# A DLRM tower on one core: pair banks spread between other matmuls, and the low halves of the tables made in two pieces with waits

## Chip, core and metric

The kernel runs on one core of a Trainium2 chip. The metric is the device time of one execution in microseconds (us). Five engines work side by side, each through its own list of instructions: TensorE (PE), VectorE (DVE), ScalarE (ACT), GpSimd (POOL) and SyncE (SP). They wait for one another through semaphores.

## What is computed

For 2048 samples, 27 embedding rows of 128 floats are looked up, the 351 dot products of each sample's rows are taken, 16 dense features are put behind them, and a small network of three layers follows.

```python
e = jnp.stack([tbl_0[ids[:, 0]], ..., tbl_26[ids[:, 26]]], axis=1)   # 2048 x 27 x 128
xactions = jnp.einsum('bfd,bgd->bfg', e, e)
z = xactions[:, _TRIL_I, _TRIL_J].reshape(2048, -1)                   # 351 pairs
h = jnp.concatenate([z, dense_ctx], axis=1)                           # 367
h = jnp.maximum(h @ W_top1 + b_top1, 0.0)                             # 512
h = jnp.maximum(h @ W_top2 + b_top2, 0.0)                             # 256
y = h @ W_top3
```

The tables have 1000, 1250, 12500 or 125000 rows.

## The kernel before

The 2048 samples are 16 tiles of 128, in 8 groups of 2 tiles (256 samples). A group passes through these steps; the list `STEPS`, written out by `order()` (L66), sets their order on every engine.

- **hot**: the 10 or 11 smallest tables are looked up by matmuls. Each such table lies in SBUF in chunks of 128 rows (8 chunks for the first five, 10 for the others). VectorE makes a one-hot matrix of 128 x 256 for each chunk (`make_one_hots`, L763) and TensorE multiplies it with the chunk (`look_up`, L510 and L511). For full precision a table is held as a high part and a low part, and each chunk takes two matmuls. ScalarE makes the high part (`make_high`, L632) and VectorE the low part, as table minus high part (`make_low`, L738). Both are made once, during group 0: for each table VectorE makes the low part and then the one-hots of group 0, in two halves, the second of which waits for the first (`hot_made`). The one-hots go into a ring of 20.
- **cold**: the other tables' rows are fetched from HBM by GpSimd, one indirect DMA for a tile and a table (L471, 260 in all), transposed by TensorE four at a time (L493), and copied by ScalarE (L639) into `et`, where the hot results go too (L651).
- **pairs**: the dot products of 64 samples are one "pair bank" of 64 matmuls of 26 columns (`row_pairs`, L526). A group has 4 pair banks, which use two PSUM banks in turn: a bank may start when the bank before the last has been moved out. Each bank has 4 strips, which ScalarE and VectorE copy out in shares set by `strips_of` (L410), 4 copies to a strip. The banks 0 and 1 need tile 0 of the group, 2 and 3 need tile 1.
- **layer1, layer2, layer3** of the group before: 12 (L540), 8 (L559) and 4 (L576) matmuls, with ScalarE's relus between (L657, L666). Before layer1 some of the pair results are moved to their places by DMAs that SyncE issues (`complete_zt`, L369), 14 and one for the dense features. For the last group they are split by tile between SyncE and GpSimd (8 and 7 or 7 and 8 for a tile), and layer1 runs tile by tile (L550).

An fp32 matmul of the program is two records in the trace, each with a weight load, so a pair bank is 128 matmul records and 128 loads. In group 0 there is no earlier group, and tile 1's cold steps and the pair banks 1 to 3 come among the first hot steps of group 1. In the last group the layer1 of the group before stands among the pair banks.

## Time and profile before

| | us |
|---|---|
| median of 3 executions | 388.83 |
| lowest, highest | 386.91, 1133.02 |
| the profiled execution | 386.78 |
| its span, first to last instruction | 385.0 |
| PE, DVE, ACT, POOL busy | 351.8, 272.6, 231.8, 274.3 |

The profiled execution lies 2 us under the median of the three and 0.1 under the lowest. The span misses 1.8 us of its time, which lie ahead of the first and behind the last instruction. Times in the rows below count from the start of the span. An idle time stands in brackets behind a row, with what ended it; "issue" says that the profile shows nothing that the engine waited for.

### The profile page before, as it was taken

What the parts mean: (1) busy time and instruction counts of PE and PEld (TensorE: products, weight loads), DVE (VectorE), ACT (ScalarE), POOL (GpSimd) and SP (SyncE); (2) the same over time, 40 slices, a digit from 0 to 9 for tenths busy, and PEclk for the clock granted to TensorE, in tenths of its full rate; (3) what the DMA queues carried; (4) which work ended last, traced back from release to release, by engine and by line L of the source; (5) the groups of instructions that cost most, each with busy time, mean ns of one, the idle gap of its engine ahead of it and who ended that gap; (6) DMA issues with size and microseconds to landing.
All of it is one profiled execution on the core that took longest, in us unless ns stands there. A gap on an engine that the chain in (4) does not pass through costs nothing.

```text
span 385.0 us, 15124 instructions
## 1 busy us (share of the span) xinstructions
PE 351.8 (91%) x6340; PEld 327.9 (85%) x6340; DVE 272.6 (71%) x1052; ACT 231.8 (60%) x504; POOL 274.3 (71%) x283
## 2 busy tenths in 40 slices
PE   0857796999999999999999999999999999998798
PEld 0856685998899989998999989998889989997687
DVE  2999997794679827894779737894679938894421
ACT  3468255944658465754768465753848555777543
POOL 4878877777777777777777777777777777783340
PEclk9999999999999999999999999999999999999899
DMA  7977243253132533225232533234222512221000
GB/s 267 382 226 232 72 135 112 82 173 93 50 85 56 165 85 78 59 63 152 51 84 53 155 83 81 55 76 161 55 82 54 159 52 58 52 60 32 8 10 2
DMA packets 20675, 38.39 MB, mean 100 GB/s; under 512 B 7040, under 2 KB 9536, under 8 KB 20608
## 3 DMA queue, kind: packets, MB, share of 16 engines
q0 software_dynamic: 8800, 17.12, 16.8%
q1 hardware_dynamic: 9824, 17.42, 13.9%
q10 hardware_dynamic: 1984, 2.89, 2.3%
q8 instruction: 50, 0.82, 0.9%
q14 instruction: 17, 0.14, 0.1%
HBM read 36.53 MB, written 0.01 MB: 95 GB/s over the span
## 4 chain that ended last, share of the span: by engine, by line
PE 66%; POOL 13%; issue 8%; DVE 6%; DMA 3%; SPq 3%; ACT 1%; DVEq 0%
PE fill_ps L510 15%; PE fill_ps L511 15%; POOL rows L471 13%; PE pair_ps L526 11%; PE mlp_ps L540 9%; PE fill_ps L493 5%; PE mlp_ps L559 5%; DVE one_hot L763 4%; SPq L369 3%; DVE table_lo L738 2%; DMA work<-tbl_d 2%; PE fill_ps L550 1%; DMA rows<-tbl_d,ids_sb 1%; PE mlp_ps L510 1%; PE mlp_ps L511 1%
## 5 line engine op out<-in xcount | busy, mean ns | idle before, releaser
L471 POOL DMA_INDIRECT rows<-tbl_d,ids_sb x260 | 265.9, 1023 | 82.8 <-issue 75.9
L763 DVE TENSOR_SCALAR one_hot<-hot_ids 128x256 fp32r<-128x256 f32 x780 | 187.1, 304 | 25.1 <-PE fill_ps L511 13.4
L510 PE MATMUL fill_ps<-one_hot,table_hi 128*128 128x256 f32 x748 | 187.2, 290 | 16.3 <-DVE one_hot L763 16.0
L511 PE MATMUL fill_ps<-one_hot,table_lo 128*128 128x256 f32 x748 | 182.8, 285 | 0.0
L510 PEld LDWEIGHTS fill_ps<-one_hot,table_hi 128*128 128x128 f32 x748 | 144.6, 193 | 18.1 <-issue 15.5
L511 PEld LDWEIGHTS fill_ps<-one_hot,table_lo 128*128 128x128 f32 x748 | 144.8, 194 | 0.2
L410 ACT COPY work<-pair_ps 26x112 f32<-26x112 f32 (+1 forms) x280 | 66.7, 238 | 51.7 <-PE pair_ps L526 48.6
L410 DVE COPY work<-pair_ps 26x112 f32<-26x112 f32 (+1 forms) x168 | 43.3, 258 | 52.2 <-PE pair_ps L526 50.2
L639 ACT COPY et<-fill_ps 128x512 f32<-128x512 f32 (+1 forms) x68 | 75.2, 1241 | 4.2 <-PE fill_ps L493 3.9
L651 ACT COPY et<-fill_ps 128x512 f32<-128x512 f32 (+1 forms) x44 | 49.6, 1161 | 43.1 <-PE fill_ps L511 39.3
L526 PEld LDWEIGHTS pair_ps<-et 128*26 128x26 f32 x4096 | 45.6, 103 | 23.5 <-issue 15.0
L526 PE MATMUL pair_ps<-et 128*26 128x26 f32 x4096 | 54.2, 192 | 12.1 <-issue 6.3
L540 PE MATMUL mlp_ps<-work,w_sb 128*128 128x256 f32 x168 | 39.2, 390 | 0.2 <-DMA work<-dense_d 0.2
L493 PE MATMUL fill_ps<-ident,rows 128*128 128x128 f32 x260 | 35.4, 276 | 2.8 <-ACT et L651 1.3
L540 PEld LDWEIGHTS mlp_ps<-work,w_sb 128*128 128x128 f32 x168 | 32.3, 196 | 4.8 <-DMA work<-dense_d 0.4
L493 PEld LDWEIGHTS fill_ps<-ident,rows 128*128 128x128 f32 x260 | 28.7, 141 | 4.3 <-DMA rows<-tbl_d,ids_sb 3.6
L748 DVE TENSOR_SCALAR hot_ids<-hot_ids,first_row 128x512 f32<-128x512 int32 (+1 forms) x54 | 23.8, 452 | 3.9 <-DMA hot_ids<-ids_hot_d 3.9
L559 PE MATMUL mlp_ps<-work,w_sb 128*128 128x256 f32 x112 | 26.3, 379 | 0.0
L657 ACT ACTIVATE work<-mlp_ps,vectors 128x256 f32<-128x256 f32 x28 | 11.8, 471 | 23.5 <-PE mlp_ps L540 23.5
L559 PEld LDWEIGHTS mlp_ps<-work,w_sb 128*128 128x128 f32 x112 | 20.3, 190 | 2.3
L369 POOL DMA_DIRECT2D hot_ids<-hot_ids x14 | 7.1, 514 | 15.1 <-ACT hot_ids L410 10.9
L410 DVE COPY hot_ids<-pair_ps 26x112 f32<-26x112 f32 (+1 forms) x32 | 8.3, 258 | 11.9 <-PE pair_ps L526 11.5
(41 smaller groups left out, 112.4 us busy)
## 6 DMA issues: line engine op xcount, KB each, us to landing
hot_ids<-ids_hot_d SPq DMA_DIRECT2D x34, 256.0 KB, 4.1
rows<-tbl_d,ids_sb POOLq DMA_INDIRECT x260, 4.1
work<-tbl_d SPq DMA_DIRECT2D x5, 640.0 KB, 4.1
work<-tbl_d SPq DMA_DIRECT2D x4, 512.0 KB, 7.2
hot_ids<-ids_hot_d ACTq DMA_DIRECT2D x6, 256.0 KB, 7.2
w_sb<-w_d ACTq DMA_DIRECT2D x5, 256.0 KB
hot_ids<-ids_hot_d SPq DMA_DIRECT2D x6, 128.0 KB, 3.9
w_sb<-tbl_d SPq DMA_DIRECT2D x1, 640.0 KB, 4.0
```

The costliest lines, as they stand in the source:

```text
L410: last = copy(homes_of_pairs[g][STRIP * q:STRIP * q + PAIR_COLS, place(q + 1)[1]:, at:at + BANK_ROWS], frm[:, q::STRIPS, :])
L471: nc.gpsimd.indirect_dma_start(out=rows[:, t, c, :], out_offset=None, in_=tables[f], in_offset=bass.IndirectOffsetOnAxis(ap=ids_sb[:, tile ...
L493: last = nc.tensor.transpose(bank[:, c * P:(c + 1) * P], rows[:, t, c0 + c, :], ident[:, :])
L510: nc.tensor.matmul(to, table_hi[:, CHUNK_AT[k] + c, :], hot, start=(c == 0), stop=False)
L511: last = nc.tensor.matmul(to, table_lo[:, CHUNK_AT[k] + c, :], hot, start=False, stop=(c == CHUNKS_OF[k] - 1))
L526: last = nc.tensor.matmul(pair_ps[bank % 2][32 * s:32 * s + PAIR_COLS, r * PAIR_COLS:(r + 1) * PAIR_COLS], et[:, row, 0:FEATURES - 1], et[ ...
L540: last = nc.tensor.matmul(mlp_psum(m), w1_sb[:, c, m * P:(m + 1) * P], zt[g][:, c, :], start=(c == 0), stop=(c == CHUNKS - 1))
L559: last = nc.tensor.matmul(mlp_ps[m][:, 0:COLS], w2_sb[:, c, m * P:(m + 1) * P], h1[:, c, :], start=(c == 0), stop=(c == K2 - 1))
L639: nc.scalar.copy(et[:, t * P:(t + 1) * P, c0:c0 + n].rearrange("p r f -> p f r"), fill_psum(step)[:, 0:n * P].rearrange("p (f r) -> p f r" ...
L651: nc.scalar.copy(et[:, :, slot:slot + n].rearrange("p r f -> p f r"), fill_psum(step)[:, 0:n * COLS].rearrange("p (f r) -> p f r", f=n)).t ...
L748: nc.vector.tensor_scalar(ids.bitcast(F32), ids, first_row[:, n:n + 1], None, ALU.subtract).then_inc(hot_ids_local, 1)
L763: last = nc.vector.tensor_scalar(one_hot[:, (first + c - c0) % ONE_HOT_RING, :], ids, float(c), None, ALU.is_equal)
```

## The change

It has three parts.

1. `order()`: the steps are written so that no two pair banks follow one another. In group 0, hot step 1 of group 1 moves from between the cold steps to between pair banks 2 and 3. In the last group, the layer1 of the group before is cut into four steps of 3 matmuls, one behind each pair bank; before, it was two steps of 6, behind banks 1 and 3. Layer1 is called by quarters in the other groups too, where the order stays as it was; it signals `h1_full` four times rather than twice, and ScalarE's relus wait for the same matmuls as before.
2. `strips_of`: in the last group bank 1 is shared 2 and 2 strips, where VectorE had 1 and ScalarE 3.
3. `make_low`: each table's low part is made in two halves. VectorE waits ahead of the first until its one-hots so far are finished, between the halves until the first is finished, and behind them until the second is finished. The count of `lo_made` doubles for all who wait on it.

```diff
         if b == 0:
-            steps += [hot[0]] + first_cold[:2] + [("pairs", b, 1), first_cold[2], hot[1]] + first_cold[3:]
-            steps += [("pairs", b, 2), ("pairs", b, 3)]
+            steps += [hot[0]] + first_cold[:2] + [("pairs", b, 1)] + first_cold[2:]
+            steps += [("pairs", b, 2), hot[1], ("pairs", b, 3)]
...
         else:
-            steps += cold[1] + [("pairs", g, 0), ("pairs", g, 1), ("layer1", b, 0), ("pairs", g, 2), ("pairs", g, 3)]
-            steps += [("layer1", b, 1), ("layer2", b, 0), ("layer2", b, 1)]
+            steps += cold[1]
+            for bank in range(PAIR_BANKS):
+                steps += [("pairs", g, bank), layer1[bank]]
+            steps += [("layer2", b, 0), ("layer2", b, 1)]
...
-        shares = {"dve": (3, 1, 2, 2), "act": (1, 3, 2, 2)}
+        shares = {"dve": (3, 2, 2, 2), "act": (1, 2, 2, 2)}
...
-                nc.vector.tensor_tensor(table_lo[:, c0:c1, :], raw_table(k), table_hi[:, c0:c1, :].bitcast(F32),
-                                        ALU.subtract).then_inc(lo_made, 1)
+                for half, (c0, c1) in enumerate(halves(k)):
+                    at = slice(CHUNK_AT[k] + c0, CHUNK_AT[k] + c1)
+
+                    wait_count(dve, hot_made, 2 * min(k, N_HOT[0]))
+                    wait_count(dve, lo_made, 2 * k + half)
+                    nc.vector.tensor_tensor(table_lo[:, at, :], raw_table(k)[:, c0:c1, :],
+                                            table_hi[:, at, :].bitcast(F32), ALU.subtract).then_inc(lo_made, 1)
+                wait_count(dve, lo_made, 2 * k + 2)
```

On TensorE, in the last group, these rows stood between the last transposes and the tile-by-tile layer1 (`pair_ps` are the two banks of the pairs, `mlp_ps` those of the layers):

```order
L526 MATMUL pair_ps0<-et 26x26 x64
L526 MATMUL pair_ps1<-et 26x26 x64
L540 MATMUL mlp_ps0<-work,w1_sb 128x256 x6
L526 MATMUL pair_ps0<-et 26x26 x64
L526 MATMUL pair_ps1<-et 26x26 x64
L540 MATMUL mlp_ps1<-work,w1_sb 128x256 x6
L559 MATMUL mlp_ps0<-work,w2_sb 128x256 x4
L559 MATMUL mlp_ps1<-work,w2_sb 128x256 x4
```

and these stand there now:

```order
L529 MATMUL pair_ps0<-et 26x26 x64
L542 MATMUL mlp_ps0<-work,w1_sb 128x256 x3
L529 MATMUL pair_ps1<-et 26x26 x64
L542 MATMUL mlp_ps0<-work,w1_sb 128x256 x3
L529 MATMUL pair_ps0<-et 26x26 x64
L542 MATMUL mlp_ps1<-work,w1_sb 128x256 x3
L529 MATMUL pair_ps1<-et 26x26 x64
L542 MATMUL mlp_ps1<-work,w1_sb 128x256 x3
L560 MATMUL mlp_ps0<-work,w2_sb 128x256 x4
L560 MATMUL mlp_ps1<-work,w2_sb 128x256 x4
```

The matmuls are the same; every bank has 3 of layer1 behind it.

On TensorE, in group 0, these rows stood between pair bank 1 and hot step 2 of group 1 (hot step 1, which writes `mlp_ps1`, is 16 chunks of two rows each, of which the first is shown):

```order
L526 MATMUL pair_ps1<-et 26x26 x64
L493 MATMUL fill_ps0<-ident,rows 128x128 x4
L510 MATMUL mlp_ps1<-one_hot,table_hi 128x256
...
L493 MATMUL fill_ps1<-ident,rows 128x128 x4
L493 MATMUL fill_ps2<-ident,rows 128x128
L526 MATMUL pair_ps0<-et 26x26 x64
L526 MATMUL pair_ps1<-et 26x26 x64
```

and now:

```order
L529 MATMUL pair_ps1<-et 26x26 x64
L496 MATMUL fill_ps0<-ident,rows 128x128 x4
L496 MATMUL fill_ps1<-ident,rows 128x128 x4
L496 MATMUL fill_ps2<-ident,rows 128x128
L529 MATMUL pair_ps0<-et 26x26 x64
L513 MATMUL mlp_ps1<-one_hot,table_hi 128x256
...
L529 MATMUL pair_ps1<-et 26x26 x64
```

The 9 transposes of tile 1 stand together, and the hot step has moved behind pair bank 2.

On VectorE, in the start, one table of 10 chunks was (`hot_ids` are the ids that a one-hot is made from; each instruction's waits stand behind it):

```order
L738 TENSOR_TENSOR table_lo<-work,table_hi 128x1280 [waits hi_made,raw_in2]
L763 TENSOR_SCALAR one_hot<-hot_ids 128x256 [waits hot_made,hot_used,hot_ids_local]
L763 TENSOR_SCALAR one_hot<-hot_ids 128x256 x4
L763 TENSOR_SCALAR one_hot<-hot_ids 128x256 [waits hot_made,hot_used]
L763 TENSOR_SCALAR one_hot<-hot_ids 128x256 x4
```

and are now:

```order
L744 TENSOR_TENSOR table_lo<-work,table_hi 128x640 [waits hot_made,lo_made,hi_made,raw_in2]
L744 TENSOR_TENSOR table_lo<-work,table_hi 128x640 [waits lo_made,hot_made]
L770 TENSOR_SCALAR one_hot<-hot_ids 128x256 [waits hot_used,hot_made,hot_ids_local,lo_made]
L770 TENSOR_SCALAR one_hot<-hot_ids 128x256 x4
L770 TENSOR_SCALAR one_hot<-hot_ids 128x256 [waits hot_made,hot_used]
L770 TENSOR_SCALAR one_hot<-hot_ids 128x256 x4
```

One subtraction has become two of half its width, and the first one-hot now waits for `lo_made` as well.

## Rows read from the trace of the kernel before

**Rows 1.** The page: busy time and instructions, and the queue that loads instructions.

```profile
PE 351.8 (91%) x6340; PEld 327.9 (85%) x6340; DVE 272.6 (71%) x1052; ACT 231.8 (60%) x504; POOL 274.3 (71%) x283
...
q8 instruction: 50, 0.82, 0.9%
```

**Rows 2.** Busy time by stretch: length, then us and count for PE, PEld, DVE, ACT, POOL.

```profile
271.00:314.00 43.00, 42.48 (x788) 39.78 (x787) 31.54 (x127) 26.30 (x59) 32.94 (x34) 1.00 0.30 83
```

**Rows 3.** Waits: who for whom, us in total, times, longest.

```profile
PE fill_ps L510 <- DVE one_hot L763: 16.0, 5, 10.5
```

**Rows 4.** Timeline of VectorE in the start: start, us, engine, line, operation.

```profile
24.80 1.48 DVE L738 TENSOR_TENSOR table_lo<-work,table_hi 128x1280 fp32r<-128x1280 f32 x1
26.20 2.46 DVE L763 TENSOR_SCALAR one_hot<-hot_ids 128x256 fp32r<-128x256 f32 x10
28.58 1.48 DVE L738 TENSOR_TENSOR table_lo<-work,table_hi 128x1280 fp32r<-128x1280 f32 x1
...
46.30 0.70 DVE L786 MEMSET work<- 128x768 f32 x1 [0.23 <-PE fill_ps L511]
```

**Rows 5.** Groups of instructions by form: busy us, mean ns, idle before.

```profile
L738 DVE TENSOR_TENSOR table_lo<-work,table_hi 128x1024 fp32r<-128x1024 f32 x4 | 4.9, 1237 | 2.6 <-ACT table_hi L632 2.6
```

**Rows 6.** Timeline of GpSimd in the start.

```profile
28.65 2.22 POOL L471 DMA_INDIRECT rows<-tbl_d,ids_sb  x1 [0.30 <-issue]
31.18 0.94 POOL L471 DMA_INDIRECT rows<-tbl_d,ids_sb  x1 [0.30 <-issue]
```

**Rows 7.** Timeline of TensorE: the two waits for a gather after the start.

```profile
99.11 0.66 PE L493 MATMUL fill_ps<-ident,rows 128*128 128x128 f32 x4 [0.24 <-DMA rows<-tbl_d,ids_sb]
...
351.88 0.66 PE L493 MATMUL fill_ps<-ident,rows 128*128 128x128 f32 x4 [0.29 <-DMA rows<-tbl_d,ids_sb]
```

**Rows 8.** Timeline of TensorE: pair banks 2 and 3 of group 0.

```profile
62.81 2.64 PE L526 MATMUL pair_ps<-et 128*26 128x26 f32 x189 [1.41 <-ACT et L639]
67.55 0.92 PE L526 MATMUL pair_ps<-et 128*26 128x26 f32 x67 [2.10 <-issue]
68.40 0.38 PE L510 MATMUL fill_ps<-one_hot,table_hi 128*128 128x256 f32 x1
```

**Rows 9.** Timeline of ScalarE ahead of them: the cold copies of tile 1.

```profile
53.83 1.22 ACT L639 COPY et<-fill_ps 128x512 f32<-128x512 f32 x1 [2.39 <-PE fill_ps L493]
54.80 1.27 ACT L639 COPY et<-fill_ps 128x512 f32<-128x512 f32 x1
58.61 1.22 ACT L639 COPY et<-fill_ps 128x512 f32<-128x512 f32 x1
61.34 1.43 ACT L639 COPY et<-fill_ps 128x512 f32<-128x512 f32 x2 [1.51 <-PE fill_ps L493]
```

**Rows 10.** Timeline of TensorE: the pair banks of the last group.

```profile
352.46 2.04 PE L526 MATMUL pair_ps<-et 128*26 128x26 f32 x214
356.89 0.71 PE L526 MATMUL pair_ps<-et 128*26 128x26 f32 x42 [2.40 <-issue]
357.53 4.22 PE L540 MATMUL mlp_ps<-work,w_sb 128*128 128x256 f32 x12
361.69 2.72 PE L526 MATMUL pair_ps<-et 128*26 128x26 f32 x201
365.60 0.65 PE L526 MATMUL pair_ps<-et 128*26 128x26 f32 x55 [1.19 <-issue]
366.18 2.86 PE L540 MATMUL mlp_ps<-work,w_sb 128*128 128x256 f32 x12
```

**Rows 11.** PE by stretch: length, busy, granted clock (share of 2.4 GHz), DMA.

```profile
354.50:356.90 2.40, 0.01 (x1) 1.00 0.01 3
356.90:360.30 3.40, 3.40 (x49) 0.50 0.02 5
```

**Rows 12.** Timeline of all engines: behind the last pair bank, up to the last tile's layer1.

```profile
368.70 5.17 SPq L369 DMA_DIRECT2D hot_ids<-hot_ids  x7
...
375.63 2.94 PE L550 MATMUL fill_ps<-hot_ids,w_sb 128*128 128x128 f32 x24
```

More of the change, by code:

```diff
@@ L94, in order @@
         steps += [hot[2]] + cold[0][:2] + [hot[3]] + cold[0][2:4] + hot[4:] + cold[0][4:]
+        layer1 = [("layer1", b, m) for m in range(HIDDEN1 // P)]
         if g < LAST:
-            steps += [("layer1", b, 0), ("layer1", b, 1), ("pairs", g, 0)] + cold[1][:2] + [("layer2", b, 0)]
+            steps += layer1 + [("pairs", g, 0)] + cold[1][:2] + [("layer2", b, 0)]
             steps += [("pairs", g, 1)] + cold[1][2:] + [("layer2", b, 1)]
         else:
-            steps += cold[1] + [("pairs", g, 0), ("pairs", g, 1), ("layer1", b, 0), ("pairs", g, 2), ("pairs", g, 3)]
-            steps += [("layer1", b, 1), ("layer2", b, 0), ("layer2", b, 1)]
+            steps += cold[1]
+            for bank in range(PAIR_BANKS):
+                steps += [("pairs", g, bank), layer1[bank]]
+            steps += [("layer2", b, 0), ("layer2", b, 1)]
     return steps
@@ L416, in load_table @@
             def load_table(k):
-                wait_count(sp, lo_made, k - RAW_SLOTS + 1)
+                wait_count(sp, lo_made, 2 * (k - RAW_SLOTS + 1))
                 sp.dma_start(raw[k % RAW_SLOTS][:, 0:CHUNKS_OF[k] * DIM],
@@ L502, in look_up @@
                         pe.wait_ge(hi_made, k + 1)
-                        pe.wait_ge(lo_made, k + 1)
+                        pe.wait_ge(lo_made, 2 * (k + 1))
                     to = bank[:, (k - k0) * COLS:(k - k0 + 1) * COLS]
@@ L529, in row_pairs, with layer1 @@
                 last.then_inc(pair_full, 1)
-            def layer1(g, half):
-                if half == 0:
+            def layer1(g, m):
+                if m == 0:
                     if g == 0:
@@ L537, in layer1 @@
                     wait_count(pe, y_done, g)
-                for m in range(half * K2 // 2, (half + 1) * K2 // 2):
-                    for c in range(CHUNKS):
-                        last = nc.tensor.matmul(mlp_psum(m), w1_sb[:, c, m * P:(m + 1) * P], zt[g][:, c, :],
-                                                start=(c == 0), stop=(c == CHUNKS - 1))
+                for c in range(CHUNKS):
+                    last = nc.tensor.matmul(mlp_psum(m), w1_sb[:, c, m * P:(m + 1) * P], zt[g][:, c, :],
+                                            start=(c == 0), stop=(c == CHUNKS - 1))
                 last.then_inc(h1_full, 1)
@@ L551, in layer1_last @@
                                                 zt[LAST][:, c, t * P:(t + 1) * P], start=(c == 0), stop=(c == CHUNKS - 1))
-                    if m % 2 == 1:
-                        last.then_inc(h1_full, 1)
+                    last.then_inc(h1_full, 1)
             def layer2(g, m):
@@ L619, in load_weights @@
                     c = step[3]
-                    act.wait_ge(lo_made, MOST_HOT)
+                    act.wait_ge(lo_made, 2 * MOST_HOT)
                     act.dma_start(w1_sb[:, c, :], w1[c * P:(c + 1) * P, :]).then_inc(w_in, 16)
@@ L655, in relu1 @@
             def relu1(g, m):
-                act.wait_ge(h1_full, g * (K2 // 2) + m // 2 + 1)
+                act.wait_ge(h1_full, g * K2 + m // 2 * 2 + 2)
                 nc.scalar.activation(h1[:, m, :], mlp_psum(m), ACT.Relu, bias=b1_sb[:, m:m + 1]).then_inc(h1_done, 1)
             def relu1_last(t, m):
-                act.wait_ge(h1_full, (LAST + t) * (K2 // 2) + m // 2 + 1)
+                act.wait_ge(h1_full, (LAST + t) * K2 + m // 2 * 2 + 2)
                 nc.scalar.activation(h1[:, m, t * P:(t + 1) * P], h1_last_psum(t, m), ACT.Relu,
@@ L715, in _ @@
                         act.wait_ge(w_in, 16 * N_W)
-                    for m in range(step[2] * K2 // 2, (step[2] + 1) * K2 // 2):
-                        relu1(step[1], m)
+                    if step[2] % 2 == 1:
+                        relu1(step[1], step[2] - 1)
+                        relu1(step[1], step[2])
                 elif step[0] == "layer2":
@@ L784, in _ @@
                 make_low(k)
-            dve.wait_ge(lo_made, MOST_HOT)
+            dve.wait_ge(lo_made, 2 * MOST_HOT)
             nc.vector.memset(zt[0], 0.0).then_inc(zt_clear, 1)
```

1 line of the change is left out of this document (removed).

## The prediction

> **What bounds the kernel now.** I read the busy times first: TensorE works 351.8 of 385.0 us, more than any other engine [rows 1]. The busy times by stretch say when: in a stretch of the middle it is busy 42.48 of 43 us [rows 2], and it is like that from 68 us to 350. So the middle is worth nothing but its own matmuls, which the change leaves alone. TensorE is idle in three places, and only there can time go or come.
>
> - The start, up to 47 us. TensorE waits for one-hots, 16.0 us in 5 waits [rows 3], while VectorE works without a gap: low part, one-hots, low part [rows 4]. VectorE's own sum sets the end of the start.
> - Pair banks 2 and 3 of group 0, with waits of 1.41 for ScalarE's copies and 2.10 us put down to "issue" [rows 8].
> - The last group, from 352 us: waits of 2.40 and 1.19 us, again inside pair banks and put down to "issue" [rows 10].
>
> GpSimd is the second suspect: its gathers follow one another with 0.30 us between, and the last one lands just before TensorE needs it. But TensorE waits for gathers only 0.24 and 0.29 us after the start [rows 7].
>
> **What the "issue" waits are.** There are 12680 matmuls and loads on TensorE and 50 transfers on the instruction queue, 16 KB and so about 254 instructions each [rows 1]. A pair bank is 256 instructions. In the last group 214 matmuls with their loads run, 428 instructions in 2.04 us, and then TensorE stands 2.40 us; later 201 run, then 1.19 [rows 10]; in group 0, 189, then 2.10 [rows 8]. That fits two loaded blocks run dry: 428 is 256 and a rest of 172. The rest ends after 86 matmuls, at 353.3; the next block is there at 356.9, 3.6 us later. The same working for the second wait (of a new block 42 pair matmuls and 12 of layer1 are spent, which leaves 74) gives about 3.1 us. I take 3.4 us from an emptied block to a new one. Single banks with slow work between them show no such wait.
>
> By the Trainium skill, "Runtime: NRT & Kernel Launch", section Instruction fetch mechanics, TensorE holds 2048 instructions and is refilled in blocks of 256, mostly hidden. The block size agrees with the 16 KB of the queue; the capacity does not agree with a wait after 428 instructions. Held to its capacity, two banks in a row would not run dry and spreading them would give nothing; that is rival B below.
>
> **Part 3, the halved low parts (the start).** Before, from one table's subtraction to its first one-hot is 1.40 us (24.80 to 26.20), less than the 1.48 it takes, since the next instruction starts under its end; the same holds for the subtraction behind one-hots (26.20 + 2.46 = 28.66, start at 28.58) [rows 4]. A width of 1280 takes 1.48 and of 1024 1.24 [rows 4, 5], about 1.0 ns an element, so half of 1280 takes about 0.83 and half of 1024 0.71. Two halves are 0.19 and 0.18 more than one whole. To it come the waits: each turns an overlap of 0.08 into a gap. For the gap the nearest row is the memset that waits for the last low part, 0.23 us behind it, with two separate wait instructions [rows 4]. The built-in wait of the one-hots shows less: ten one-hots take 2.46 where ten at 0.20 would take 2.10, so a boundary costs 0.27 to 0.36 in all, overlap and signal included. I take 0.23 for the gap ahead of the first half (several waits), 0.11 between the halves, 0.04 behind the second (its wait is the last one in the order and the others are already met). A table of 1280 then takes 0.83 + 0.11 + 0.83 + 0.04 = 1.81 where it took 1.40, +0.41; one of 1024 the same. The wait ahead of the first half adds 0.31 for the 4 tables with no id subtraction in front (tables 2, 4, 6, 8); for the 5 others that work covers it. Ten tables: 10 x 0.41 + 4 x 0.31 = **+5.3 us**. Table 10 comes behind the last one-hot of group 0 and its 0.7 us are covered, since the next one-hots are ready over 1 us early. Nothing hides the rest: VectorE has no idle time there, and behind it TensorE waits, then ScalarE's last copy, then the first pair bank. Below: every gap at 0.04 and the first wait at 0.12, +3.9. Above: every gap at the memset's 0.23, +0.73 a table and 4 x 0.31, +8.5.
>
> What it gives: GpSimd's gather that starts at 28.65, just behind a subtraction's start, takes 2.22 us, the next one 0.94 [rows 6]; it ends 0.8 us behind the subtraction. Nine gathers of the start are stretched like this, 7.2 us in all. By the Trainium skill, "SBUF — State Buffer", section Who interferes with whom, a VectorE instruction with two SBUF inputs shuts out a GpSimd instruction that reads SBUF until it is finished. The row agrees. With halves a gather is held for 0.8 us at most, and I would expect GpSimd to win back about half of the 7.2. But TensorE, now later by 5.3, can take of that only its own two waits, 0.24 + 0.29 [rows 7]: **-0.5 us**.
>
> **Part 1 in group 0.** Hot step 1 covered ScalarE's copies of tile 1. Now 9 transposes stand together and pair bank 2 waits for three copies in a row. In the old times: ScalarE starts the first at 58.61 as before, and its copies start 0.97 apart (53.83 to 54.80), the short last one takes 0.5 [rows 9]. So they end at 58.61 + 1.94 + 0.5 = 61.1, and bank 2 starts then, not at 62.81. With 1.6 for it, 3.9 for the hot step and 1.7 for bank 3 without a wait, the stage ends at 68.3, before 68.40 [rows 8]: **-0.1 us**. The 2.10 is saved and the idle time ahead of bank 2 grows from 1.41 to 3.7. That has a price: behind the idle 2.40 us at 354.5 the clock is 1.2 GHz for 3.4 us and comes back then [rows 11], while behind the idle 2.10 [rows 8] it stayed at 2.4. At 1.2 GHz the 12 matmuls of layer1 take 4.22 instead of 2.86, 1.4 us more [rows 10]. I charge **+1.3 us** (0 to 1.7).
>
> **Parts 1 and 2 in the last group.** From the first bank, S = 352.46. By the 214 matmuls in 2.04 us a bank runs 1.25 us when its instructions are loaded; half of layer1's 12 in 2.86, less the tail of the last, is 1.3 at full clock [rows 10]. With a block 3.4 us behind an emptied one, and 172 instructions of the first block left at S, I get waits of about 0.9 in bank 1 and 0.9 in bank 3, both too short for a low clock. Bank 3 then ends at 4 x 1.25 + 3 x 1.3 + 1.8 = S + 10.7; before, it ended at 366.25, or S + 13.8, of which 0.1 is the last matmul's tail. So it ends 3.0 us sooner. What follows it stays: the copies, 2.45 us from the bank's end to SyncE's first DMA at 368.70, seven DMAs in 5.17 us, their landing, and the last tile's layer1 at 375.63 [rows 12]. SyncE must be free for them. It is, just: bank 1 ends at about S + 4.7 and 8 copies on ScalarE, in place of 12, follow, so its 8 DMAs for tile 0 run from about S + 7.2 to S + 13.0, and bank 3's copies end at S + 13.2. TensorE is through with layer1, layer2 and the first tile's layer1 by about S + 19.1; the DMAs set the last tile's start, S + 20.2 instead of S + 23.2: **-3.0 us** (-1.5 if one wait of 2.4 stays; -4.5 if the waits vanish and SyncE's DMAs for tile 0 are through sooner too). Part 2 serves only to free SyncE in time.
>
> **Sum.** 5.3 - 0.5 - 0.1 + 1.3 - 3.0 = +3.0 us on the profiled execution's 386.78: 389.8. Against the median of the runs shown, 388.83, that is 0.2% more; against the lowest, 386.91, 0.7%. 2% is about what a measurement of this kernel can tell from no change.
>
> **Rivals.**
> A. The waits are all but free. By the Trainium skill, "VectorE: DVE Perf Modes", section The DRAIN you can't avoid, a semaphore between VectorE operations costs nothing extra. The overlap of 0.08 that the rows show [rows 4] speaks against it. Priced by rows: only the second instruction's 0.19 a table less that overlap, about +1.0 in all, gives 386.8 + 1.0 - 0.5 - 0.1 + 1.3 - 3.0 = 385.5. Chance 0.15.
> B. The waits inside pair banks stay, because they come from elsewhere than the number of instructions in a row. Then the last group gives 0, and 386.8 + 5.3 - 0.5 - 0.1 + 1.3 = 392.8. For it: no row names the cause, and how much is loaded ahead is worked out, not seen. Against: all three long waits stand in the second bank of a pair of banks. Chance 0.12.
> C. Slower by more than forecast, by one mechanism, the start. If each of the three waits of a table costs what the memset shows, the start grows by 8.5 and the time is 393.0. From 4.3 us on (388.83 - 386.78 + 0.5 + 0.1 - 1.3 + 3.0) the kernel is slower than the old median. For it: three separate wait instructions stand there. Against: most are met long before. Chance 0.18.
> D. The gathers were the bound in the background, and freeing them gives more than 0.53. Then the start's growth would be hidden by 3 to 4 us and the time is about 386.3. Against: TensorE has no idle time that they could fill. Chance 0.05.
> The forecast has 0.50.
>
> **The numbers.** 389.8, range 385.4 to 393.4: it takes in B and C at their price and A at its edge. Faster by over 2% (under 381.1) would need A, the full 4.5 and more: 0.02. Slower by over 2% (over 396.6) would need B and C together and a low clock in the start: 0.05. Within 2%: 0.93.
>
> **What would show it.** Start: the first pair bank at about 52.7 instead of 47.4; subtractions of 0.83 us with gaps behind them; gathers of at most 1.7 us. Group 0: an idle time of 3 to 4 us ahead of bank 2, a clock of 0.5 behind it, no idle time over 0.3 inside bank 3. Last group: idle times inside banks under 1 us, no low clock, the last tile's layer1 20 us behind the first bank. If the first pair bank is not late, part 3 is priced wrongly; if banks still stand 2 us, the reading of "issue" is wrong.

## The result, and the profile after

| | before | after |
|---|---|---|
| median of the runs side by side, us | 387.87 | 391.67 |
| lowest, highest | 386.73, 1133.02 | 391.50, 392.89 |
| the profiled execution | 386.78 | 391.63 |
| its span | 385.0 | 389.8 |

The ratio is 1.0119, with a 95% interval of 1.0082 to 1.0156: slower, but by less than 2%. The forecast was 389.8 with a range of 385.4 to 393.4. The time lies in it, on the side of the slower rivals. The 1133.02 is a single execution of the kernel before, far outside all its others, and the ratio leaves it out.

The parts of the span, from the timelines of TensorE in both traces:

| part | before | after | difference | forecast |
|---|---|---|---|---|
| up to the first pair bank | 47.44 | 52.57 | +5.1 | +5.3 |
| from there to hot step 2 of group 1 | 20.96 | 23.46 | +2.5 | +1.2 |
| from there to the first bank of the last group (S) | 284.07 | 283.27 | -0.8 | -0.5 |
| from S to the last tile's layer1 | 23.17 | 21.18 | -2.0 | -3.0 |
| from there to the end | 9.33 | 9.33 | 0 | 0 |
| sum | | | +4.8 | +3.0 |

The page of the kernel after, with the busy times first and then the granted clock in 40 slices:

```profile
PE 353.3 (91%) x6340; PEld 328.9 (84%) x6340; DVE 278.3 (71%) x1067; ACT 231.0 (59%) x500; POOL 268.4 (69%) x283
...
PEclk9998998899999999999999999999999999999999
```

TensorE works 1.5 us more than in [rows 1]. VectorE works 5.7 us more, GpSimd 5.9 less. VectorE's work counts in the start, where TensorE waits for it. In the middle TensorE is still the bound, so that neither VectorE's nor GpSimd's time matters there (length, busy us and count of PE, PEld, DVE, ACT, POOL; 42.24 of 43, against 42.48 in [rows 2]):

```profile
271.00:314.00 43.00, 42.24 (x786) 39.43 (x785) 31.19 (x125) 27.20 (x62) 32.78 (x34) 1.00 0.32 87
```

The start. First TensorE's waits for one-hots (us in all, times, longest; 16.0 in 5 in [rows 3]), then VectorE's timeline, then GpSimd's:

```profile
PE fill_ps L513 <- DVE one_hot L770: 20.9, 8, 10.7
```

```profile
27.35 1.74 DVE L744 TENSOR_TENSOR table_lo<-work,table_hi 128x640 fp32r<-128x640 f32 x2
29.13 2.34 DVE L770 TENSOR_SCALAR one_hot<-hot_ids 128x256 fp32r<-128x256 f32 x10
31.67 1.75 DVE L744 TENSOR_TENSOR table_lo<-work,table_hi 128x640 fp32r<-128x640 f32 x2 [0.20 <-DVE one_hot L770]
```

```profile
30.74 0.94 POOL L474 DMA_INDIRECT rows<-tbl_d,ids_sb  x1 [0.30 <-issue]
31.99 1.32 POOL L474 DMA_INDIRECT rows<-tbl_d,ids_sb  x1 [0.30 <-issue]
```

From a table's first half to its first one-hot it is 29.13 - 27.35 = 1.78 us; in [rows 4] it was 1.40. The last one-hot ends at 31.47 and the next half starts 0.20 later, where the subtraction of before started 0.08 ahead of that end. The longest gather of the start is 1.49 us, where it was 2.23, and all of them together are stretched beyond 0.94 us by 3.9 us in place of 8.1.

Group 0 on TensorE: pair bank 1 in two pieces, the transposes of tile 1, banks 2 and 3 (the hot step between them is left out):

```profile
59.17 1.45 PE L529 MATMUL pair_ps<-et 128*26 128x26 f32 x105
62.11 0.36 PE L529 MATMUL pair_ps<-et 128*26 128x26 f32 x23 [1.49 <-issue]
62.40 1.20 PE L496 MATMUL fill_ps<-ident,rows 128*128 128x128 f32 x9
67.05 1.96 PE L529 MATMUL pair_ps<-et 128*26 128x26 f32 x128 [3.44 <-ACT et L640]
...
74.28 1.82 PE L529 MATMUL pair_ps<-et 128*26 128x26 f32 x128
```

Bank 3 runs whole: its 2.10 of [rows 8] is gone. The idle time ahead of bank 2 is 3.44 where it was 1.41. TensorE by stretch (length, busy and count, granted clock, DMA share, GB/s) shows a low clock that lasts from 65.1 to 71.9, the first 2 us of it while TensorE still stood idle:

```profile
65.20:68.40 3.20, 1.35 (x105) 0.50 0.62 213
68.40:71.90 3.50, 3.50 (x56) 0.50 0.24 61
72.00:76.00 4.00, 3.88 (x148) 1.00 0.21 53
```

The last group on TensorE, which answers to [rows 10]:

```profile
359.30 1.27 PE L529 MATMUL pair_ps<-et 128*26 128x26 f32 x128
360.49 1.56 PE L542 MATMUL mlp_ps<-work,w_sb 128*128 128x256 f32 x6
361.99 0.87 PE L529 MATMUL pair_ps<-et 128*26 128x26 f32 x80
363.35 0.60 PE L529 MATMUL pair_ps<-et 128*26 128x26 f32 x48 [0.50 <-issue]
363.88 1.56 PE L542 MATMUL mlp_ps<-work,w_sb 128*128 128x256 f32 x6
365.37 0.80 PE L529 MATMUL pair_ps<-et 128*26 128x26 f32 x73
367.11 0.65 PE L529 MATMUL pair_ps<-et 128*26 128x26 f32 x55 [0.94 <-issue]
367.69 1.56 PE L542 MATMUL mlp_ps<-work,w_sb 128*128 128x256 f32 x6
369.18 0.75 PE L529 MATMUL pair_ps<-et 128*26 128x26 f32 x67
370.95 0.70 PE L529 MATMUL pair_ps<-et 128*26 128x26 f32 x61 [1.01 <-issue]
```

Three waits, 2.45 us in all, in place of two of 3.59, and no low clock. Count the instructions between them, two to a matmul record: from S to the first wait 2 x (128 + 6 + 80) = 428, then 2 x (48 + 6 + 73) = 254, then 2 x (55 + 6 + 67) = 256. Before, the first wait came after 428 too, and the second after 2 x (42 + 12 + 201) = 510. The waits stand at the same places of the instruction list, every 254 to 256; the matmuls were moved past them.

### The profile page after: what moved, and what is told of

It is laid out like the page before. It is cut to its first block, busy times and chain, and to the rows that moved or that the text cites. A ratio compares the mean times of both kernels' runs of the same rounds, so it can differ in the third digit from the quotient of the medians.

```text
span 389.8 us, 15164 instructions
## 1 busy us (share of the span) xinstructions
PE 353.3 (91%) x6340; PEld 328.9 (84%) x6340; DVE 278.3 (71%) x1067; ACT 231.0 (59%) x500; POOL 268.4 (69%) x283
## 4 chain that ended last, share of the span: by engine, by line
PE 83%; DVE 9%; issue 3%; ACT 2%; DMA 1%; DVEq 0%; SPq 0%; ACTq 0%
PE fill_ps L513 21%; PE fill_ps L514 21%; PE pair_ps L529 13%; PE mlp_ps L542 9%; PE fill_ps L496 7%; PE mlp_ps L560 6%; DVE one_hot L770 5%; DVE table_lo L744 4%; DMA work<-tbl_d 1%; PE fill_ps L552 1%; PE mlp_ps L513 1%; PE mlp_ps L514 1%; PE mlp_ps L577 1%; ACT et L640 1%; ACT hot_ids L413 0%
## 5 line engine op out<-in xcount | busy, mean ns | idle before, releaser
L474 POOL DMA_INDIRECT rows<-tbl_d,ids_sb x260 | 260.0, 1000 | 82.8 <-issue 78.3
L770 DVE TENSOR_SCALAR one_hot<-hot_ids 128x256 fp32r<-128x256 f32 x780 | 189.5, 306 | 30.6 <-PE fill_ps L514 14.0
L513 PE MATMUL fill_ps<-one_hot,table_hi 128*128 128x256 f32 x748 | 188.3, 292 | 21.7 <-DVE one_hot L770 20.9
L513 PEld LDWEIGHTS fill_ps<-one_hot,table_hi 128*128 128x128 f32 x748 | 144.9, 194 | 24.0 <-issue 20.6
L542 PEld LDWEIGHTS mlp_ps<-work,w_sb 128*128 128x128 f32 x168 | 31.1, 190 | 4.1
L755 DVE TENSOR_SCALAR hot_ids<-hot_ids,first_row 128x512 f32<-128x512 int32 (+1 forms) x54 | 22.9, 435 | 3.9 <-DMA hot_ids<-ids_hot_d 3.9
L658 ACT ACTIVATE work<-mlp_ps,vectors 128x256 f32<-128x256 f32 x28 | 11.8, 471 | 21.6 <-PE mlp_ps L542 21.5
L560 PEld LDWEIGHTS mlp_ps<-work,w_sb 128*128 128x128 f32 x112 | 20.2, 190 | 3.1 <-ACT work L658 0.9
L744 DVE TENSOR_TENSOR table_lo<-work,table_hi 128x640 fp32r<-128x640 f32 (+1 forms) x18 | 13.8, 766 | 4.4 <-ACT table_hi L633 2.6
```

The costliest lines, as they stand in the source:

```text
L474: nc.gpsimd.indirect_dma_start(out=rows[:, t, c, :], out_offset=None, in_=tables[f], in_offset=bass.IndirectOffsetOnAxis(ap=ids_sb[:, tile ...
L513: nc.tensor.matmul(to, table_hi[:, CHUNK_AT[k] + c, :], hot, start=(c == 0), stop=False)
L542: last = nc.tensor.matmul(mlp_psum(m), w1_sb[:, c, m * P:(m + 1) * P], zt[g][:, c, :], start=(c == 0), stop=(c == CHUNKS - 1))
L560: last = nc.tensor.matmul(mlp_ps[m][:, 0:COLS], w2_sb[:, c, m * P:(m + 1) * P], h1[:, c, :], start=(c == 0), stop=(c == K2 - 1))
L744: nc.vector.tensor_tensor(table_lo[:, at, :], raw_table(k)[:, c0:c1, :], table_hi[:, at, :].bitcast(F32), ALU.subtract).then_inc(lo_made, 1)
L770: last = nc.vector.tensor_scalar(one_hot[:, (first + c - c0) % ONE_HOT_RING, :], ids, float(c), None, ALU.is_equal)
```

## The experiments

Two theories stood against each other at each of three places. Start: the waits cost, or the halving does. Last group and group 0: "issue" is the supply of instructions, or something tied to pair banks. Cost behind an idle time: the idle time itself, or the low clock that it brings. The runs e5 to e8 were executed once each, and such a time tells little, as most executions of the kernel before lie anywhere from 384.28 to 389.91 us. What e5 to e8 show is read from their profiles. The parts of each profile, in us (P0 is the first pair bank; "low clock" lists the stretches at a granted clock of 0.5 that do not lie wholly in the first 45 us):

| kernel | P0 | P0 to hot step 2 | to S | S to last layer1 | span | low clock |
|---|---|---|---|---|---|---|
| before | 47.4 | 21.0 | 284.1 | 23.2 | 385.0 | 356.9-360.3 |
| after | 52.6 | 23.5 | 283.3 | 21.2 | 389.8 | 65.1-71.9 |
| e1 halves | 53.0 | 20.2 | 283.7 | 23.0 | 389.2 | 362.0-365.4 |
| e2 no halves | 47.5 | 22.7 | 283.5 | 21.7 | 384.7 | 59.2-66.1 |
| e3 last only | 48.0 | 20.8 | 285.2 | 21.5 | 384.8 | 69.3-72.7 |
| e4 group 0 only | 48.2 | 22.7 | 282.2 | 23.5 | 385.9 | 59.2-66.0, 366.4-369.8 |
| e5 halves, no waits | 48.6 | 21.1 | 284.5 | 20.9 | 384.4 | 69.5-73.0 |
| e6 whole, waits | 52.6 | 19.9 | 284.2 | 23.0 | 389.1 | 47.5-50.9, 361.5-364.9 |
| e7 half banks | 47.7 | 20.2 | 283.1 | 19.3 | 379.6 | 359.2-362.6 |
| e8 kept busy | 53.9 | 22.3 | 282.4 | 20.5 | 388.4 | none |
| e11 spread wide | 51.0 | 20.7 | 281.6 | 22.1 | 384.7 | none |
| e12 three early | 50.0 | 16.8 | 286.5 | 20.6 | 383.2 | none |

In e11 the first bank of the last group lies ahead of half of the transposes (8, 1.0 us), and in e12 hot step 2 ahead of bank 3, so that their middle columns are not to be set against the others. What can be compared for all is the stretch from P0 to the last tile's layer1: 328.2 before, 327.9 after, 327.5 in e3, 324.4 in e11 and 323.9 in e12. In e1, e5 and e6, which have the order of before, it is 326.9, 326.5 and 327.1, so that a difference of under 2 says nothing. In the last two P0 itself was late, by 3.5 and 2.6, though their start has the instructions of before. Two transposes there waited for gathers, and the clock fell during these waits and stayed low for 6.8 us (35.6-42.4 in e11, 33.8-40.6 in e12).

**e1: part 3 alone.** The kernel before, with `make_low` of the change.

```diff
...
+                    wait_count(dve, hot_made, 2 * min(k, N_HOT[0]))
+                    wait_count(dve, lo_made, 2 * k + half)
+                    nc.vector.tensor_tensor(table_lo[:, at, :], raw_table(k)[:, c0:c1, :],
...
```

> Part 3 alone, the kernel before otherwise. Theory (VectorE's own sum sets the start): first pair bank at 52.5 (47.4 before), waits for gathers after the start gone (-0.5 to -0.9), the rest as before; 391.4 us, +4.5. Rival (relief of GpSimd's gathers pays for it): first pair bank as late, but the span from there to the last group shortens by 3 us or more; 388.5 or less.

Measured: 391.25 us, 1.0122 (1.0077 to 1.0167). P0 is 5.5 later than before, and the rest is nearly as before: from P0 to S it is 303.9, 1.1 shorter, and not the 3 of the rival. This part alone is as slow as the whole change.

**e2: parts 1 and 2 without part 3.** The change, with `make_low` of before.

```diff
-                for half, (c0, c1) in enumerate(halves(k)):
...
+                nc.vector.tensor_tensor(table_lo[:, c0:c1, :], raw_table(k), table_hi[:, c0:c1, :].bitcast(F32),
...
```

> The changed kernel with the low parts made whole again, so parts 1 and 2 alone. Theory: first pair bank at 47.4, group 0's stage +2.5 us longer than before (low clock, longer wait inside bank 1), last group 2.0 us shorter; 387.3 us, +0.5. Rival (the parts act together: GpSimd's stretched gathers come late for the transposes that now stand together): a wait for gathers of over 1 us in group 0 and a time over 389.

Measured: 386.21 us, 0.9979 (0.9957 to 1.0001): at best a gain of 0.4%. The two ratios multiplied give 1.010, the whole change 1.012. Group 0 again has a long idle time ahead of bank 2 and the low clock behind it, from 59.2 to 66.1, and a wait of 0.44 for a gather appears among its transposes (another, of 0.73, lies in the start):

```profile
58.11 0.33 PE L496 MATMUL fill_ps<-ident,rows 128*128 128x128 f32 x1 [0.44 <-DMA rows<-tbl_d,ids_sb]
61.14 2.12 PE L529 MATMUL pair_ps<-et 128*26 128x26 f32 x128 [2.70 <-ACT et L640]
```

**e3: the last group alone** (the layer1 quarters and the shares of part 2).

```diff
+            steps += cold[1]
+            for bank in range(PAIR_BANKS):
+                steps += [("pairs", g, bank), layer1[bank]]
...
```

> Only the last group's order and its shares, everything else as in the kernel before. Theory: from first bank to the last tile's layer1 21.2 us instead of 23.2, rest as before; 384.8 us, -2.0. Rival (the wait for instruction blocks only moves): 23 us there and 386.8.

Measured: 386.02 us, 0.9984 (0.9956 to 1.0013). S to the last layer1 is 1.7 shorter than before, the span 0.2. What lies between is not the change's doing. TensorE waits longer for gathers, 3.1 us in three waits (0.5 in two before), 2.9 of them in the start, where P0 is 0.6 later. And the clock was low from 69.3 to 72.7, behind the wait of 1.83 in bank 3 of group 0, so that hot step 2 took 6.06 where it took 4.57 before. The waits for blocks stand at the same matmuls as in the kernel after: 0.71 ahead of the last 48 of bank 1, then 1.02 and 1.01.

**e4: group 0 alone.**

```diff
-            steps += [hot[0]] + first_cold[:2] + [("pairs", b, 1), first_cold[2], hot[1]] + first_cold[3:]
-            steps += [("pairs", b, 2), ("pairs", b, 3)]
+            steps += [hot[0]] + first_cold[:2] + [("pairs", b, 1)] + first_cold[2:]
+            steps += [("pairs", b, 2), hot[1], ("pairs", b, 3)]
```

> Only group 0's new order, everything else as in the kernel before. Theory: idle 3.4 us ahead of bank 2 instead of 1.4, 2.1 us wait inside bank 3 gone, clock at 1.2 GHz for 3.4 to 6.8 us behind the idle; the stage 1.5 to 2.5 us longer than before, 388.8 us. Rival (the low clock is chance and does not come here): stage as long as before or 0.1 shorter, 386.7.

Measured: 387.74 us, 1.0022 (0.9996 to 1.0048). In the profile the stage of group 0 is 1.7 longer than before; in the times no loss is clear. The expectation was 388.8.

**e5: halves without a wait.** Part 3 with its three `wait_count` lines left out; the instructions of VectorE stay in their order.

```diff
-                    wait_count(dve, hot_made, 2 * min(k, N_HOT[0]))
-                    wait_count(dve, lo_made, 2 * k + half)
...
-                wait_count(dve, lo_made, 2 * k + 2)
```

> The kernel before with the low parts in two halves, without the added waits. Theory (the waits are most of the price): 0.11 us a table dearer than whole (two instructions of 0.82, each with the usual overlap of 0.08), first pair bank at 48.5; gathers of the start stretched as before, up to 2.2 us, since VectorE leaves no gap. Rival (the second instruction is the price): first pair bank at 50 or later.

Measured: 386.27 us (one run; before beside it 389.70). P0 is 48.6, 1.2 later than before and 4 to 4.4 sooner than with the waits. VectorE's timeline has no gaps, and the gathers of the start are stretched as ever, by 8.3 us in all (8.1 before, 3.9 after), one of them by more than any before:

```profile
29.58 1.55 DVE L739 TENSOR_TENSOR table_lo<-work,table_hi 128x640 fp32r<-128x640 f32 x2
31.05 2.42 DVE L764 TENSOR_SCALAR one_hot<-hot_ids 128x256 fp32r<-128x256 f32 x10
```

```profile
34.29 2.87 POOL L471 DMA_INDIRECT rows<-tbl_d,ids_sb  x1 [0.30 <-issue]
```

From the first half to the first one-hot it is 1.47, 0.07 more than for the whole subtraction. So halving as such costs little, and it is the waits that both cost the time and let GpSimd in. The last group of this kernel has the old order, and it is the most telling of all, because its clock did not drop:

```profile
354.25 2.04 PE L526 MATMUL pair_ps<-et 128*26 128x26 f32 x214
358.09 0.54 PE L526 MATMUL pair_ps<-et 128*26 128x26 f32 x42 [1.80 <-issue]
358.56 2.86 PE L540 MATMUL mlp_ps<-work,w_sb 128*128 128x256 f32 x12
361.35 2.02 PE L526 MATMUL pair_ps<-et 128*26 128x26 f32 x201
365.09 0.65 PE L526 MATMUL pair_ps<-et 128*26 128x26 f32 x55 [1.73 <-issue]
```

Bank 3 ends at 365.74, that is S + 11.5; in the new order it ended at S + 12.35 (after). In e1, with the same order, the clock fell behind the first wait, of 2.33, and the first half of layer1 took 4.54 in place of 2.86.

**e6: whole low parts with the waits around them.**

```diff
+                wait_count(dve, hot_made, 2 * min(k, N_HOT[0]))
+                wait_count(dve, lo_made, k)
                 nc.vector.tensor_tensor(table_lo[:, c0:c1, :], raw_table(k), table_hi[:, c0:c1, :].bitcast(F32),
+                wait_count(dve, lo_made, k + 1)
```

> The kernel before with whole low parts and the waits ahead of and behind each. Theory: per table +0.12 behind and +0.3 ahead where no id subtraction stands in front; 10 x 0.12 + 4 x 0.3 = +2.4, first pair bank at 49.9; gathers stretched less than before, since a gap ahead lets one in, 2.2 us ones rare. Rival (waits are free): first pair bank at 47.4 to 47.7.

Measured: 390.91 us (one run; before beside it 389.70), P0 52.65. I had expected P0 to move by 2.4, and it moved by 5.2. The waits' share is 1.12 behind the subtractions and 1.55 ahead of them, which is the 2.4 expected and a little more:

```profile
31.02 1.49 DVE L740 TENSOR_TENSOR table_lo<-work,table_hi 128x1280 fp32r<-128x1280 f32 x1 [0.20 <-DVE one_hot L766]
32.55 1.70 DVE L766 TENSOR_SCALAR one_hot<-hot_ids 128x256 fp32r<-128x256 f32 x6
```

Its one-hots took 1.1 us more than before, and TensorE's matmuls on the last table ran at the low clock from 47.5 to 50.9, which cost 1.5 (4.13 us in place of 2.6). Why the one-hots took longer stays open.

**e7: half pair banks in the last group.** Old order. Half of the last group's pair matmuls are left out.

```diff
-                for r in range(BANK_ROWS):
+                for r in range(BANK_ROWS // 2 if g == LAST else BANK_ROWS):
```

> The kernel before, last group only: each pair bank does 8 of its 16 rows, 32 matmuls instead of 64, and leaves the others out; order and copies unchanged. Theory (instruction blocks run dry): two such banks in a row are 256 instructions and no wait over 0.3 us comes inside them; clock stays high; first bank to layer1's first half 2.6 us instead of 5.1. Rival (the wait comes from the alternation of PSUM banks or the copies): a wait of about 2.4 us stays in the second bank.

Measured: 381.39 us (one run). Two half banks in a row, 256 instructions, run without a wait, and so does the second pair of them but for a true wait for a copy. Layer1's first half starts 1.24 us behind the first bank, sooner than the 2.6 expected, and the clock did not stay high as expected: it fell behind that wait for the copy.

```profile
350.94 1.32 PE L526 MATMUL pair_ps<-et 128*26 128x26 f32 x128
352.18 2.86 PE L540 MATMUL mlp_ps<-work,w_sb 128*128 128x256 f32 x12
355.16 0.72 PE L526 MATMUL pair_ps<-et 128*26 128x26 f32 x64
358.09 0.72 PE L526 MATMUL pair_ps<-et 128*26 128x26 f32 x64 [2.21 <-ACT hot_ids L410]
```

So it is the number of instructions, not two banks next to one another, that makes the "issue" waits. By the Trainium skill, "Runtime: NRT & Kernel Launch", section Instruction fetch mechanics, TensorE holds 2048 instructions. That does not agree: it stood after 428 in each old order, and the same old order with 256 did not.

**e8: the kernel after, TensorE kept busy ahead of bank 2.** 14 matmuls that nobody reads (28 records) fill the idle time of group 0.

```diff
+                if (g, bank) == (0, 2):
+                    for _ in range(14):
+                        nc.tensor.matmul(mlp_ps[1][:, 0:P], ident[:, :], ident[:, :], start=True, stop=True)
```

> The changed kernel with 14 spare matmuls of 128 columns into an unused PSUM bank ahead of pair bank 2 of group 0, where TensorE was idle 3.4 us. Theory (the idle time costs the clock): clock stays at 2.4 GHz, hot step 1 takes 4.1 instead of 5.4 us, from the first pair bank to hot step 2 22.0 instead of 23.5 us; 390.2. Rival (the low clock comes from the waits inside the banks): clock falls all the same, 391.6.

Measured: 390.26 us (one run; before beside it 389.70).

```profile
64.76 3.29 PE L524 MATMUL mlp_ps<-ident 128*128 128x128 f32 x28
68.45 2.06 PE L532 MATMUL pair_ps<-et 128*26 128x26 f32 x128 [0.41 <-ACT et L643]
```

```profile
68.50:76.20 7.70, 7.40 (x288) 6.76 (x288) 3.93 (x16) 3.79 (x16) 5.87 (x7) 1.00 0.22 59
```

Bank 2 starts 14.5 us behind P0, as in the kernel after, since it waits for ScalarE's copies; but the clock stays at 2.4 GHz (1.00 in the row), the hot step takes 4.10 instead of 5.42, and the stage 22.3 instead of 23.5. So the idle time itself was covered by what bank 2 waited for, and the low clock behind it was the avoidable part, 1.2 us. Bank 2 itself took 2.06 here, at full clock, and 1.96 in the kernel after, at the low one: the price was paid in the hot step alone. The span is 1.4 shorter than that of the kernel after, with a P0 1.4 later, but 1.6 of it lie in the middle and the last group, and that part is not shown to come from the spare matmuls.

The last group of this kernel tests the count of instructions once more. The 28 spare records are 56 instructions with their loads, and the first wait comes after 2 x (128 + 6 + 52) = 372 instructions from S, 56 fewer than the 428 of the other kernels with whole banks; the next two follow after 254 and 256:

```profile
361.31 0.64 PE L532 MATMUL pair_ps<-et 128*26 128x26 f32 x52
362.27 0.83 PE L532 MATMUL pair_ps<-et 128*26 128x26 f32 x76 [0.33 <-issue]
```

**e9 and e10: two other orders, at a time when everything was slow.** All kernels took some 570 us in these runs, the one before too (575.77), where the same chip, by its number, had run e5 to e8 and the kernel before in 381 to 391 us some eight minutes earlier. e9 is written like e11 and e10 like e12, below.

> As e3 (only the last group changed), but with the two halves of the last transposes put behind pair banks too: 8 transposes, bank 0, 8 transposes, bank 1, two quarters of layer1, bank 2, a quarter, bank 3, a quarter. Theory (blocks of instructions arrive every 3.7 us there, so the sum of the waits is set by how many instructions there are, not by their order): waits inside the banks 1.5 to 2.7 us in sum, from the last hot matmul to the last tile's layer1 as in e3 within 1 us; 385 to 386. Rival (distance between banks is what counts): waits under 0.5 us in sum and 2 us less than e3, 384.

> As e3, and in group 0 hot step 1 stays where it was (it covers ScalarE's copies) while hot step 2 goes between pair banks 2 and 3. Theory: idle 1.4 us ahead of bank 2 as before, no wait over 0.3 inside bank 3, no low clock there; from the first pair bank to the end of hot step 2 about 2 us less than before; 384.4, ahead of both kernels. Rival (ScalarE's later copies of hot step 2 hold up the PSUM ring): a new wait of 2 us or more in front of the next transposes or hot step, 386 or more.

Measured: 573.26 and 572.10, ratios 0.985 (0.964 to 1.005) and 0.996 (0.989 to 1.003). They can't tell the orders apart. In e9 136 us of TensorE's waits are put down to "issue", most of them in the pair banks (us in total, times, longest):

```profile
PE pair_ps L528 <- issue: 94.9, 125, 1.9
```

These are 125 waits where the instruction queue moved 50 blocks, so they do not stand one to a block as above. What slowed these executions is not shown.

**e11: spread wider in the last group.** e3's kernel, but with cold steps between banks 0 and 1 and a half of layer1 behind bank 1.

```diff
...
+            steps += cold[1][:2] + [("pairs", g, 0)] + cold[1][2:] + [("pairs", g, 1)] + layer1[:2]
+            steps += [("pairs", g, 2), layer1[2], ("pairs", g, 3), layer1[3]]
...
```

> The kernel of e9 again, since that time both it and the kernel before stood at 570 us, with instruction loading slow throughout. Theory: waits inside the last group's banks 1.5 to 2.7 us in sum; 385 to 386. Rival (distance between banks counts): under 0.5 us in sum; 384.

Measured: 385.34 us, 0.994 (0.990 to 0.998). It is the only kernel here that is clearly faster than before. Its waits inside banks stand where the instruction count puts them (444 from S, of which 16 are the 8 transposes that now lie behind S, then 510), and add up to 2.76:

```profile
357.64 0.54 PE L528 MATMUL pair_ps<-et 128*26 128x26 f32 x42 [1.20 <-issue]
...
366.07 0.70 PE L528 MATMUL pair_ps<-et 128*26 128x26 f32 x61 [1.56 <-issue]
```

These are no shorter than e3's 2.74. Its profiled execution took 386.53 and does not show the gain as a whole: its start was 3.5 later, with two waits for gathers in it, 3.9 in all, and the low clock. From P0 to the last layer1 it is 3.8 shorter than before, and 2.1 shorter than any kernel with the order of before and whole banks. Its interval and that of e3 (0.9956 to 1.0013) overlap, and they were run on different chips, so that it is faster than e3 is not shown either.

**e12: three hot steps ahead of bank 3 in group 0.** e3's last group, hot step 1 back at its old place, and hot step 2 of group 1 moved between banks 2 and 3.

```diff
...
-            steps += [("pairs", b, 2), ("pairs", b, 3)]
+            steps += [("pairs", b, 2), hot[2], ("pairs", b, 3)]
...
```

> The kernel of e10 again, for the same reason. Theory: idle 1.4 us ahead of bank 2 of group 0, no wait over 0.3 us inside bank 3, about 2 us less than before from the first pair bank to the end of hot step 2; 384.4. Rival: a new wait of 2 us or more in front of the next transposes or hot step; 386 or more.

Measured: 386.16 us, 0.998 (0.995 to 1.0009). Bank 2 waits only 1.40 and bank 3 not at all:

```profile
65.06 1.81 PE L529 MATMUL pair_ps<-et 128*26 128x26 f32 x128 [1.40 <-ACT et L640]
...
71.30 1.75 PE L529 MATMUL pair_ps<-et 128*26 128x26 f32 x128
```

So the 2.10 can be had without the long idle time. From P0 to S it is 303.3 where it was 305.0 before, but e7, with the old steps there, has 303.3 too, so that this gain is not clear of the spread. To the last layer1 it is 4.3 less than before. The span shows 1.8 of them, since the start is 2.6 later, with two waits for gathers of 4.7 in all:

```profile
34.40 1.12 PE L496 MATMUL fill_ps<-ident,rows 128*128 128x128 f32 x4 [2.85 <-DMA rows<-tbl_d,ids_sb]
37.39 0.47 PE L496 MATMUL fill_ps<-ident,rows 128*128 128x128 f32 x1 [1.87 <-DMA rows<-tbl_d,ids_sb]
```

Up to there no engine has other instructions than before. Whether such a start is as frequent with the kernel before is not shown, since only one execution of each was profiled. The rival (a new wait of 2 us or more ahead of the next transposes or hot step) is false: the waits there are 0.30 to 0.41.

## Why the prediction was right, and where it was off

**The start: right, in size and in cause.** +5.1 in the profile, forecast +5.3. The gap ahead of a first half is 0.20 (forecast 0.23), between halves 0.10 (0.11), behind the second 0.03 (0.04). The halves take 0.82 and 0.69 (0.83 and 0.71). Over ten tables, from the subtractions to the one-hots it is 3.65 us more, and ahead of the subtractions 1.55 more. e1 shows that this is all of the loss (+1.2% alone), e5 that it comes from the waits (P0 within 1.2 without them), e6 that two waits a table around a whole subtraction bring 2.7, the other 2.6 of its start having other causes. One profile's start is not exact: kernels with the start of before have P0 from 47.4 to 51.0, those with waits from 52.6 to 53.9. Rival C is false with this: the gaps were 0.20, 0.10 and 0.03, not the memset's 0.23 three times, and the start grew by 5.1, not 8.5.

**Rival A, free waits: false.** By the Trainium skill, "VectorE: DVE Perf Modes", section The DRAIN you can't avoid, a semaphore between VectorE operations costs nothing extra, as measured there on a row of copies. That does not agree: here it turned an overlap of 0.08 into a gap of 0.03 to 0.20, two or three times a table, on the engine that sets the end of the start.

**The gathers: right.** Their stretch fell from 8.1 to 3.9 us, about half, and the last one ends at 344.4 instead of 350.3. The two waits of 0.24 and 0.29 are gone, and the middle is 0.8 shorter, against 0.5 forecast; but e4, with the old gathers, has a middle 1.9 shorter, so that this difference says little. Rival D is false: the growth of the start was not hidden. Its counter-argument, "TensorE has no idle time that they could fill", was read from one trace, though. In e2, e3, e4, e11 and e12, which all have the subtractions of before, TensorE waits 1.2, 3.1, 1.3, 3.9 and 4.7 us for gathers, most of it in the start, while in the four kernels with the added waits (after, e1, e6, e8) it waits for none. Whether the waits on VectorE spare TensorE these is not shown, since e5 has none either. In any case it does not pay for those waits: e1 is 1.2% slower.

**Group 0: the mechanism and the clock's price right, a wait left out.** Bank 3's wait is gone and the idle time ahead of bank 2 grew, to 3.44 (forecast 3.7), as written. The clock fell, as charged, for 6.8 us and not for the 3.4 of [rows 11], but 2 of them were idle and bank 2 took no longer for it (e8). Its price is the hot step's, 5.42 instead of 4.07, and e8 wins 1.2 back: that is the 1.3 of the forecast. What is missing is 0.9 of bank 1's wait, 1.49 where it was 0.61 before. I left it out, and the prediction's sentence that single banks show no such wait overlooked the 0.61. In the other kernels, with the same instructions of TensorE up to there, it is anything from none (e12) to 1.24 (e8), so it is chance and not the change. The last 0.4 is spread over bank 2 (1.96, forecast 1.6) and the hot step.

**The last group: -2.0 instead of -3.0, and for another reason than I gave.** The step that failed is "I get waits of about 0.9 in bank 1 and 0.9 in bank 3". There were three, 0.50, 0.94 and 1.01; and a quarter of layer1 took 1.5 us between banks, not 1.3. Bank 3 ended at S + 12.35, not S + 10.7. Behind it SyncE's first DMA starts at 374.11, 2.45 later, as forecast. But from there to the last tile's layer1 it is 6.4 us, not the 6.9 of [rows 12]: before, TensorE's matmuls came to that layer1 without an idle time from 365.60 on, so the 6.9 were their time and not the DMAs'. In the kernel after, the layer1's first weight load waits 0.24 for a DMA, so that both paths are about equally long now. This second error hides 0.6 of the first, and the layer1 stands at S + 21.2 (forecast 20.2).

What I had not seen is that the supply sets the pace in either order. New blocks arrive at 363.35, 367.11 and 370.95, 3.8 us apart, and what TensorE does with 256 instructions takes 0.60 + 1.56 + 0.80, less the overlaps, 2.8 us. Spreading moves the waits but doesn't feed TensorE sooner. e5 shows it best, in one trace: the old order at full clock has 3.53 us of waits and reaches the last layer1 at S + 20.9, the new one with 2.45 of waits at S + 21.2. The blocks came somewhat faster in e5, 3.5 us apart; with the new order and 3.56 between them (e12) it is S + 20.6, so the order itself is worth some 0.3 us. The old order loses its 2 us where its longer waits bring the clock down, 23.0 to 23.5 in before, e1, e4 and e6. The new one never did in five profiles of the full kernel's order (20.5 to 21.7). So rival B was half true: the waits come from the number of instructions (e7, e8), but they stay, 2.45 us where 1.8 was forecast and 3.59 stood before. Nearly all of the gain is the clock's, which the forecast had in its sum, with layer1 at full clock, but did not tell apart from the waits'. That the 0.6 behind bank 3 make up for a part of the miss is luck. Why a block takes 3.3 to 4.1 us to arrive stays open.

**The sum.** +3.0 forecast, +4.8 in the spans, +3.8 between the medians. Of the 1.8 that is missing, 1.0 is the last group, 1.3 group 0 with its chance part, and -0.5 the start and the middle together. The one of group 0 is mostly chance, the other is the last group's waits.

## What to carry over

A wait between instructions of the engine that sets the pace is not free even when it is already met: price it from the nearest gap in the trace, times its count, and ask first whether the engine has idle time there. Before an order is changed to remove waits put down to "issue", count the instructions between them: if they stand at equal counts, the supply is the bound and a new order only moves them. An idle time of TensorE has to be priced with the clock behind it, which cost 1.2 to 1.7 us a time here (e8, e3, e4). And one profile is one execution: compare kernels from the first point behind which they differ, since a start with the same instructions ended anywhere from 47.4 to 51.0.

## What was unexpected of the hardware

- The low clock lasts 3.4 or 6.8 us, and the length of the idle time does not tell alone whether it comes. Behind 2.32 to 2.40 us it came (before, e1, e6), behind 3.44 too. In group 0 it stayed up behind the 2.10 of before and the 1.83 of e11, and fell behind the 1.83 of e3 and the 1.78 of e5, in the same order. And in e4 the layer1 half behind a wait of 2.45 ran at full clock (2.86 us), and the next one, behind 2.06, at the low one:

```profile
357.53 0.54 PE L526 MATMUL pair_ps<-et 128*26 128x26 f32 x42 [2.45 <-issue]
358.00 2.86 PE L540 MATMUL mlp_ps<-work,w_sb 128*128 128x256 f32 x12
...
364.87 0.65 PE L526 MATMUL pair_ps<-et 128*26 128x26 f32 x55 [2.06 <-issue]
365.45 4.54 PE L540 MATMUL mlp_ps<-work,w_sb 128*128 128x256 f32 x12
```

- Gaps of 0.03 to 0.20 us on VectorE go with a shorter stretch of GpSimd's gathers in the start: 3.4 to 3.9 us in all with three waits a table (after, e1, e8), 5.9 with two (e6), 8.1 to 9.9 with none. The longest took 1.49 with three waits and 2.23 with none, and 2.87 in e5; that one ended 1.8 us behind both halves, which the halves don't explain.
- One and the same program took 389.70 us and some 576 us on the same chip within minutes; the cause is open. In e9 95 us of waits in pair banks are put down to "issue".
